# Layer 0's values directly behind its spread, the source columns behind the values, in a four-layer graph kernel

## What is computed

```python
def _L0_gnn_ref(h, adj, W, a):
    Wh = jnp.einsum('bnf,of->bno', h, W)
    a1 = a[0, :Fo]
    a2 = a[0, Fo:]
    s1 = Wh @ a1
    s2 = Wh @ a2
    e = jax.nn.leaky_relu(s1[:, :, None] + s2[:, None, :], negative_slope=ALPHA)
    mask = adj == 0
    e = jnp.where(mask, -jnp.inf, e)
    att = jax.nn.softmax(e, axis=-1)
    att = jnp.where(mask, 0.0, att)
    return jnp.einsum('bij,bjo->bio', att, Wh)
...
    h = jnp.maximum(_layernorm(x, axis=-1), 0.0)
    x = x + _L0_gnn_ref(h, adj, L0_gnn_W, L0_gnn_a)
    h = jnp.maximum(_layernorm(x, axis=-1), 0.0)
    x = x + _L1_gnn_ref(h, adj, L1_gnn_W, L1_gnn_b, L1_gnn_a)
    h = jnp.maximum(_layernorm(x, axis=-1), 0.0)
    x = x + _L2_gnn_ref(h, adj, L2_gnn_a0, L2_gnn_a1, L2_gnn_a2, L2_gnn_a3, L2_gnn_bias)
    h = jnp.maximum(_layernorm(x, axis=-1), 0.0)
    x = x + _L3_gnn_ref(h, adj, L3_gnn_weight, L3_gnn_w_ih, L3_gnn_w_hh, L3_gnn_b_ih, L3_gnn_b_hh)
```

## Time and profile before

| what | us |
| --- | --- |
| median of 3 runs | 1065.44 |
| lowest, highest | 1063.51, 1066.78 |
| the profiled execution | 1066.04 |
| its span, first to last instruction | 1063.9 |
| busy in it: PE, DVE, ACT, POOL | 954.6, 892.3, 864.0, 132.6 |

### The profile page before, as it was taken

How to read it: one execution, slowest core, us unless ns; L and a number is a source line. 1 busy time by engine, 2 the same in 40 slices (tenths; PEclk the granted TensorE clock), 3 DMA queues, 4 the chain that set the end, 5 groups by cost and what they waited for, 6 DMA issues and landing times.

```text
span 1063.9 us, 16086 instructions
## 1 busy us (share of the span) xinstructions
PE 954.6 (90%) x5024; PEld 609.6 (57%) x5024; DVE 892.3 (84%) x2710; ACT 864.0 (81%) x1860; POOL 132.6 (12%) x170
## 2 busy tenths in 40 slices
PE   4588998999989899999989899998989999998866
PEld 3455565666566566656556566656656665655443
DVE  5296989899898979899897989989897989979543
ACT  3367888979888897988888897988889798887742
POOL 1102011010202011020201201020201101010000
PEclk8558999999999999999999999999999999999989
DMA  2401204021210403121220402121030302111000
GB/s 72 109 1 39 72 11 109 11 61 52 68 51 14 106 11 77 44 60 51 56 64 10 110 11 60 60 61 51 15 105 11 79 31 61 50 40 51 1 11 10
DMA packets 42477, 52.32 MB, mean 49 GB/s; under 512 B 1296, under 2 KB 25872, under 8 KB 42384
## 3 DMA queue, kind: packets, MB, share of 16 engines
q0 software_dynamic: 16896, 25.17, 10.7%
q1 hardware_dynamic: 17040, 21.83, 6.5%
q10 hardware_dynamic: 8448, 4.20, 1.3%
HBM read 55.39 MB, written 4.19 MB: 56 GB/s over the span
## 4 chain that ended last, share of the span: by engine, by line
PE 52%; DVE 28%; ACT 10%; issue 6%; POOL 3%; DMA 0%; DVEq 0%; SPq 0%; ACTq 0%; POOLq 0%
PE l_bank L948 7%; DVE probs L642 6%; PE a_bank L981 6%; PE x_bank L1040 4%; PE a_bank L948 3%; PE h_bank L1102 3%; ACT hn L394 3%; PE r_bank L1102 3%; PE r_bank L1105 3%; DVE sess L843 3%; DVE sess L836 3%; PE h_bank L1105 3%; PE n_bank L1105 3%; DVE probs L663 3%; POOL rstd L363 2%
## 5 line engine op out<-in xcount | busy, mean ns | idle before, releaser
L663 DVE SCALAR_TENSOR_TENSOR probs<-spread,s_lift,probs 128x512 f32<-128x512 f32 x320 | 237.4, 747 | 4.0 <-DVE rmax L642 0.5
L642 DVE CUSTOM_DVE_ANT_0 probs<-spread,mask 128x512 f32<-128x512 f32 x320 | 211.8, 684 | 2.4 <-ACT spread L450 2.3
L363 POOL TENSOR_TENSOR rstd<-var_eps,power 128x4 f32<-128x4 f32 x64 | 88.0, 1375 | 882.5 <-DVE var_eps L636 603.0
L460 ACT ACTIVATE probs<-probs,shift_p 128x512 f32<-128x512 f32 x256 | 185.7, 725 | 5.7 <-DVE shift_p L659 5.7
L468 ACT ACTIVATE pT<-l_bank 128x512 f32<-128x512 f32 x256 | 151.8, 600 | 46.5 <-PE l_bank L948 46.3
L948 PEld LDWEIGHTS l_bank<-ident,probs 128*128 128x128 f32 x1024 | 124.3, 144 | 73.8 <-issue 46.0
L948 PE MATMUL l_bank<-ident,probs 128*128 128x128 f32 x1024 | 150.5, 278 | 6.1 <-ACT probs L460 5.1
L394 ACT ACTIVATE hn<-x,shift,rstd 128x128 f32<-128x128 f32 x192 | 80.5, 492 | 26.1 <-POOL shift L365 26.0
L1005 PE MATMUL l_bank<-hT,dst_rep 128*128 128x512 f32 x128 | 73.6, 658 | 12.1 <-ACT pT L468 8.5
L870 DVE SCALAR_TENSOR_TENSOR hid_n<-r_t,hid_n 128x512 f32<-128x512 f32 x48 | 33.1, 689 | 57.8 <-ACT r_t L518 57.8
L981 PE MATMUL a_bank<-values,pT 128*128 128x128 f32 x512 | 65.7, 286 | 0.7 <-ACT pT L428 0.7
(11 more groups left out here) (175 smaller groups left out, 1956.5 us busy)
## 6 DMA issues: line engine op xcount, KB each, us to landing
adjt_i<-in_adj_t SPq DMA_DIRECT2D x16, 1024.0 KB, 5.2
edges<-in_adj POOLq DMA_DIRECT2D x16, 1024.0 KB, 5.9
adj_h<-in_adj POOLq DMA_DIRECT2D x16, 512.0 KB, 7.7
xin<-in_x SPq DMA_DIRECT2D x16, 256.0 KB, 2.9
out<-out_sb ACTq DMA_DIRECT2D x16, 256.0 KB, 3.8
weights_sb<-in_weights SPq DMA_DIRECT2D x1, 840.0 KB, 4.7
```

What stands on the lines that cost most here:

```text
L363: g.tensor_tensor(rstd[n][:], var_eps[n][:], power[:], op=ALU.pow).then_inc(pool_step[n], 1)
L460: s.activation(row, row, ACT.Exp, bias=shift_p[:, head, c:c + 1], accum_out=den[:, head, c:c + 1]).then_inc(probs_ready, 1)
L642: return v.tensor_tensor_reduce(out=row, in0=spread_row, in1=mask, scale=1.0 / LIFT, scalar=-3e38, op0=ALU.subtract, op1=ALU.max, accum_ou ...
L663: v.scalar_tensor_tensor(row, spread_row, source, row, ALU.min, ALU.subtract, reverse1=True).then_inc(ready, 1)
```

## The change

The values take the place behind the spread, and the source columns come behind the values and the four maxima. The numbers of the two steps in `WHEN` are set so by hand for PE, DVE, ACT and POOL. The waits turn with it: the values wait for the copy of the spread, the source columns for the copy of the values, the first turn t0 for s_lift. Nothing is added or left out.

```diff
-A_STEPS = (["stats0", "aggr0", "mean0"] + [f"norm0_{c}" for c in range(4)] + ["rows0", "mask0", "dst0", "src0", "values0"] + [f"m{c}" for c in range(4)]
-           + ["u0", "top0", "u1", "t0", "below0", "u2", "t1", "max0", "u3", "t2", "t3", "den0", "rden0"] + [f"sum0_{c}" for c in range(4)] + ["x1"])
+A_STEPS = (["stats0", "aggr0", "mean0"] + [f"norm0_{c}" for c in range(4)] + ["rows0", "mask0", "dst0", "values0"] + [f"m{c}" for c in range(4)]
+           + ["src0", "u0", "top0", "u1", "t0", "below0", "u2", "t1", "max0", "u3", "t2", "t3", "den0", "rden0"] + [f"sum0_{c}" for c in range(4)] + ["x1"])
...
     "tensor": (
         -161384, -160485, -160485, -159329, -155547, -153489, -152800, -152684, -152179, -151882, -151425,
-        -150476, -150476, -150401, -150401, -150068, -150068, -150068, -149683, -149312, -149312, -149172,
+        -150476, -150401, -150401, -150068, -150068, -150068, -150068, -149683, -149312, -149312, -149172,
...
                 elif step == "src0":
-                    pe.wait_ge(dst0_copied, p.count(1, 1))
+                    pe.wait_ge(val0_copied, p.count(1, 1))
                     project(0, a_bank, 1, src_w[:, 0:1], src0_ready)
                 elif step == "values0":
-                    pe.wait_ge(s10_copied, p.count(1, 1))
+                    pe.wait_ge(dst0_copied, p.count(1, 1))
                     project(0, a_bank, D, w0t_sb, val0_ready)
                 elif step[0] == "t" and step[1:].isdigit():
                     c = int(step[1])
                     if c == 0:
-                        pe.wait_ge(val0_copied, p.count(1, 1))
+                        pe.wait_ge(s10_copied, p.count(1, 1))
```

## The result

The changed kernel takes 1071.08 us (median of 8 runs, 1069.73 to 1071.86), the kernel before 1065.42 us beside it (8 runs, 1063.46 to 1067.75). The ratio is 1.0051 with a 95% interval of 1.0041 to 1.0061: slower by 0.5%, 5.7 us between the medians. The forecast was 1066.7 with a range of 1062.8 to 1069.3; the time lies above the range. The profiled execution took 1071.36 us, span 1069.2 us, where before it took 1066.04 us, span 1063.9 us. The mean granted clock was 0.954 to 0.960 in all eight runs of the changed kernel; in the runs of the kernel before that stand beside the experiments it was 0.967 to 0.976, but for one run of 1075.64 us with 0.928.

What follows compares the result with a forecast made beforehand. PE held 52% of the chain that ended last, DVE 28%. Terms 0 + 0.15 + 0.5 - 0.73 + 1.35 = +1.3 us on the 1065.44 median gave 1066.7, range 1062.8 to 1069.3.

Steps and rivals of the forecast that it cites:

- Removed wait: PE's wait for s_lift before layer 0's values, 18.8 us over 15 times: slack, so removing it is worth 0.
- Rival 4: The whole wait for s_lift was on the path: 18.8 us less, 1047; chance 0.03.
- Values moved off their old place: The 8 values matmul records on PE leave 484.15 for the source columns' place at 474.48; their leaving was worth 0.
- Rival 2: Clock comes up earlier in graph 1, between 60 and 84 us: 2 to 4 us less, 1063.7; chance 0.14.
- Source columns before head 4's spread: On PE, source columns and spread end at 488.25, before L936 can start at 488.44; fits by 0.19, worth 0.
- s_lift on DVE: Behind the fourth masked maximum it costs 0 to 0.07 us in each of graphs 2 to 15; +0.5 taken.
- Rival 1: s_lift costs its full length each round, on the way to state_lo and L1120: slower, 1069.0; chance 0.17.
- Rival 3: moments starts 0.11 us earlier each round, and POOL, hn and PE with it: 1.5 less, 1064.7; chance 0.10.
- Graph 0, -0.73: Maxima done before 17, first logits at 19.95 instead of 20.68: -0.73 us, between 0 and -0.9.
- Graph 1, +1.35: Source columns come behind head 4's spread, DVE idles about 1 us for PE: +1.35, or +2.0 at low clock.

Runs made afterwards that it cites:

- e5_rest: Kernel before, with the change made in graphs 2 to 15 alone; 1072.69 us, ratio 1.0057 to the kernel before.
- e8_fill: Changed kernel plus four useless wide matmuls in graphs 1 to 15, in PE's wait before the fourth group of transposes; 1064.44 us, ratio 0.9988 to the kernel before.
- e2_thin: Kernel before, old order and waits, with layer 0's values matmuls one column wide instead of 128; 1066.36 us, ratio 1.0005.
- e1_wide: Changed kernel with the source columns' matmuls 128 columns wide from graph 1 on, same place and waits; 1068.11 us, ratio 1.0032 to the kernel before.
- e4_first: Kernel before, with the change made in graphs 0 and 1 alone; 1063.29 us, ratio 0.9983 to the kernel before.
- e11_g0: Kernel before, with the change made in graph 0 alone; 1062.74 us, ratio 0.9984 to the kernel before.
- e3_late: Changed kernel with the values back in their old place on PE, new waits kept; 1065.16 us, ratio 1.0001 to the kernel before.
- e6_both: Changed kernel with four useless wide matmuls before the fourth group of transposes and 128-column source columns; 1062.53 us, ratio 0.9970 to the kernel before.

## Why the prediction was wrong, point by point

**Removed wait, worth 0: right.** It was slack, as the chain had said. PE waits elsewhere in its place: 5.1 us for ACT's exponentials became 32.4. Rival 4 (1047) is out.

**Values moved off their old place, priced at nothing: the step that failed.** The prediction counted the time that the records take and who hides it. It took PE's other work at the durations of the trace of before, so it took for granted that the clock stays at 1.00 in the steady rounds. The runs show falls to 0.50 instead. Four of them, 6.8 us long, cost 6.45 us in the rounds; the change in graphs 2 to 15 alone costs 7.2 us (e5_rest), and wide matmuls put back into PE's wait take 6.6 us off (e8_fill). e2_thin and e8_fill show that the wide matmuls at that place held the clock; e1_wide shows that the one-column ones in front of the spread are needed as well for a long fall. Rival 2 had the clock as a mechanism, said that it could go the other way, and looked for it in graph 1 only.

**Source columns before head 4's spread, fitting by 0.19 us: right at the full clock, wrong with it low.** PE in the round of graph 8 after the change, without a fall, which answers to the earlier trace rows:

```profile
486.56 1.04 PE L941 MATMUL a_bank<-src_w,hT 128*128 128x1 f32 x8
487.47 1.10 PE L1005 MATMUL l_bank<-hT,dst_rep 128*128 128x512 f32 x2
489.23 0.66 PE L936 MATMUL x_bank<-ident,hn 128*128 128x128 f32 x4 [0.66 <-ACT hn L394]
```

L936 still waits for hn, 0.66 us (it was 0.84, and I had said about 1). In a round with a long fall src0 takes 1.51 instead of 1.04 us and the spread 2.06 instead of 1.10, and L936 comes right behind them with no wait. The four long falls cost 1.56 to 1.66 us each, 6.45 in all, which is more than the whole loss.

**s_lift on DVE, 0.07 a round, half of it on the path: size right, path wrong.** DVE in the round of graph 8 after the change, which answers to the earlier trace rows:

```profile
484.85 0.38 DVE L629 BATCH_NORM_AGGREGATE moments<-stats 128x2 f32<-128x6 f32 x4
...
489.14 0.15 DVE L682 TENSOR_SCALAR s_lift<-a_bank 128x4 f32<-128x4 f32 x1
489.21 0.68 DVE L642 CUSTOM_DVE_ANT_0 probs<-spread,mask 128x512 f32<-128x512 f32 x1
...
490.49 0.68 DVE L865 TENSOR_TENSOR state_lo<-hn,state_hi 128x512 fp32r<-128x512 f32 x1
```

It takes 0.07 us of the row (489.14 to 489.21), and from moments to state_lo are 5.64 us, before 5.57. But the seven rounds without a fall are longer by 0.006 us each, not 0.035. So +0.04 over these rounds where the sum had +0.5 for 14. The upper end of the range even took +2.0 for this term, twice its own bound of +1.0. The whole 0.14, which the prediction drew from the Trainium skill (VectorE: DVE Perf Modes, "The DRAIN you can't avoid"), is not seen either: the next instruction starts 0.07 us after s_lift. The same section says that a next instruction that is not held starts earlier. Rival 1 (1069.0), nearest to the time in number, is wrong as a mechanism. Rival 3 is wrong too: moments still starts 0.03 us behind the end of stats3 (483.95 + 0.87 = 484.82, then 484.85).

**Graph 0, -0.73: right, once traces with a like clock are compared.** DVE after the change, which answers to the earlier trace rows:

```profile
18.90 0.16 DVE L682 TENSOR_SCALAR s_lift<-a_bank 128x4 f32<-128x4 f32 x1 [2.28 <-PE a_bank L941]
19.09 0.75 DVE L663 SCALAR_TENSOR_TENSOR probs<-spread,s_lift,probs 128x512 f32<-128x512 f32 x1
```

The first logits start at 19.09 where I had 19.95 and before it was 20.68. But this pair mixes order and clock. In the ten traces with the new order in graph 0 the first logits start between 19.04 and 21.48, in the four with the old one between 19.70 and 20.71. They come early where the clock rose early for the first time (between 14.7 and 18.5 us in the fourteen traces) and PE's gate products ran at the full level; PE's order through the gate products is the same in all of them. Counted from ACT's copy of the spread, with the rise at nearly the same time: 7.22 us in the old order (before, rise at 16.75) and 6.38 in the new (e4_first, 16.79); 6.27 in the old (e2_thin, 14.81) and 5.65 in the new (changed kernel, 14.93). So the order is worth 0.84 and 0.62 us here, about the 0.73 of the sum, and the rest of the 1.6 us is clock, which differs from one execution to the next. The runs have -1.7 us for graph 0 (e11_g0, 0.9984, interval -0.7 to -2.6), with the -0.73 at the interval's edge; what the rest is, if it is real, is not shown.

**Graph 1, +1.35: the wait came, its price did not.** The row of after that answers to the earlier trace rows:

```profile
69.67 0.16 DVE L682 TENSOR_SCALAR s_lift<-a_bank 128x4 f32<-128x4 f32 x1 [1.65 <-PE a_bank L941]
```

DVE waits 1.65 us for PE, more than the 1 us forecast. Yet e4_first and e11_g0, which differ by this graph, come out alike, though with their uncertainty of some 0.9 us each the +1.35 lies at the edge of what they allow. In this trace the first logits of graph 1 come 15.25 us behind its spread on PE, before 14.84, so only 0.41 is left of it there. The clock has a part in that, as rival 2 had it for this place: from 60 to 64 us PE ran at 1.00 and had 2.01 us to do, before at 0.50 and 4.00 us. From 72 to 76 us it was the other way (0.50, before 0.85), and the 3 us of rival 2 are not there: to graph 2's spread it is 1.40 us in all. What absorbs the wait in the runs I have not shown: the clock of this stretch differs from trace to trace (graph 2's spread starts at 102.41 in e4_first, at 104.31 in the changed kernel, which has the same order up to there).

**What stays open.** Which rounds fall is not explained: the changed kernel falls in six rounds of fourteen with nearly the same work in each. Every fall between 110 and 1010 us, in all kernels, starts 15.6 to 19.3 us behind the spread, so place in the round matters, but rounds without one look alike. Each count of falls is that of one execution. Nor is it explained why the last graphs, from graph 15's spread to the end of the span, take 172.0 and 172.3 us in e1_wide and e2_thin against 168.1 to 169.5 in before, after, e3_late, e4_first and e8_fill. In these two, two falls each start between 1035 and 1056 us, e3_late and e8_fill (169.5 and 169.3 us) one short one, the others none, but what brings those about was not tried. If they are the whole difference to the kernel before, they cost e1_wide some 3.5 us and e2_thin some 4 (an estimate from 172.0, 172.3 and 168.4).

## What to carry to other kernels

A wide matmul inside a stretch where the tensor engine often waits may be what holds its clock up, as it was in this kernel; before moving it, look at what is left on PE around its old place, and after moving it, read the granted clock round by round, not only the waits and the chain. If a fall shows, cheap tests are to put useless wide matmuls into the hole and to compare the intervals of rounds with and without a fall; here that took away the loss of 0.5% in the rounds, and with the gain of the start left 0.3%. Useless matmuls in the waits of graphs 0 and 1 gave another 0.5% on e4_first (1063.29 to 1057.61) and 0.4% on e6_both (1062.53 to 1058.10). A change that goes through all rounds of a pipeline can also be tried in a part of them: here the gain was in graph 0 and the loss in graphs 2 to 15. And two traces of different kernels can differ by a clock that rose earlier in one; compare like with like before a difference is put down to the order.

## What the hardware showed that I had not expected

- The profile's busy time did not tell the stretch with a fall from the one without. Eight records of one-column matmuls take 1.05 us at 480.50 in e2_thin, the 128-column ones 1.16 us at 481.06 in e4_first; with the first the clock fell in nine rounds, with the second in none. The Trainium skill (TensorE: Matmul & The Clock Gate, Part 1) says that the gate follows how busy PE has been; by the profile PE was busy 1.99 and 2.00 us of the 3.00 in these two stretches, so these numbers do not show it.
- The clock has two levels here too, 1.00 and 0.50, and a fall lasts 3.4 or 6.8 us in the middle rounds. A long one costs the changed kernel about 1.6 us, less than the 3.3 us by which its PE records from src0 to L1120 grow (8.44 us in the round of 547 us, 5.17 in the round of graph 8 without one): the rest is taken up by PE's slack. Short ones cost little: e2_thin has nine and its rounds take 0.8 us more.
- More work on an engine made the kernel faster by 6.6 us (e8_fill against after, medians).
